# A windowed-attention transformer kernel: scores of four units made ahead of the attention loop, and the row maxima of two units taken in succession

## The reference, cut to what matters

```
x = x + attn0(layernorm(x))            # 16 heads of 16, causal over all 1024 tokens
x = x + two_layers(layernorm(x))       # DEPTH 2, this case's part
# one layer:
h = shift_token(x)
q, k, v = split(h @ wqkv)              # 8 heads of 64
q, k = rotary_xpos(l2norm(q) * qs, l2norm(k) * ks)
o = local_attention(q, k, v)           # windows of 128 tokens; each sees itself and the one before
x = x + o @ wo
h = layernorm(shift_token(x)) * lg + lb
a, g = split(h @ w1 + b1)              # 682 hidden
x = x + (a * gelu(g)) @ w2 + b2
```

## Time and profile before

| | us |
|---|---|
| median of 3 runs | 2295.97 (2294.08 to 2304.67) |
| the profiled execution: its own time | 2298.97 |
| its span, first to last instruction | 2296.1 |
| PE busy in the span | 1990.5 (87%) |
| DVE busy | 1457.9 (63%) |
| ACT busy | 1243.2 (54%) |
| POOL busy | 798.9 (35%) |

### The profile page before, as it was taken

The page is one execution under the profiler, slowest core; times in us unless marked ns, Lnnn a source line. Parts: engine busy times, 40 slices in busy tenths (PEclk is TensorE's granted clock), DMA queues, the critical chain, the costliest instruction groups (busy, mean ns, idle before and its releaser), DMA issues.

```text
span 2296.1 us, 36136 instructions
## 1 busy us (share of the span) xinstructions
PE 1990.5 (87%) x11968; PEld 1241.2 (54%) x11968; DVE 1457.9 (63%) x3942; ACT 1243.2 (54%) x2980; POOL 798.9 (35%) x663
## 2 busy tenths in 40 slices
PE   5566899999988746999999999989899999999998
PEld 3232233333322424667667667667667667667666
DVE  5457788888885435746756755746755755756754
ACT  1110666666667323754754764763754764764663
POOL 2223321122232335505505605614613613623620
PEclk9896899999999877999999999999999999999999
DMA  4645855554540552000000000011200000000000
GB/s 144 152 124 114 147 128 83 84 73 71 105 123 11 147 156 78 1 24 14 1 24 15 1 19 19 2 68 43 73 19 19 20 19 19 19 19 19 20 1 28
DMA packets 124455, 128.97 MB, mean 56 GB/s; under 512 B 50460, under 2 KB 101232, under 8 KB 123248
## 3 DMA queue, kind: packets, MB, share of 16 engines
q1 hardware_dynamic: 123696, 117.75, 22.2%
q0 software_dynamic: 576, 8.91, 1.0%
HBM read 75.51 MB, written 50.86 MB: 55 GB/s over the span
## 4 chain that ended last, share of the span: by engine, by line
PE 38%; DVE 10%; ACT 8%; issue 5%; POOL 2%; DMA 0%; DVEq 0%; SPq 0%; ACTq 0%; POOLq 0%
PE qkv_ps L1338 5%; PE s_ps L1439 4%; DVE rot_s L1886 4%; PE s_ps L1384 4%; PE pt_ps L1518 3%; PE o_ps L1518 3%; PE pt_ps L1452 3%; PE o_ps L1477 3%; ACT p_sb L1630 3%; DVE p_sb L1895 3%; PE s_ps L1397 2%; PE qkv_ps L1397 2%; PE pt_ps L1439 2%; PE o_ps L1439 2%; POOL inv_norm L1780 2%
## 5 line engine op out<-in xcount | busy, mean ns | idle before, releaser
L717 ACT ACTIVATE probs<-st_ps 128x512 f32<-128x512 f32 (+3 forms) x768 | 329.8, 494 | 166.7 <-PE st_ps L625 166.2
L1338 PE MATMUL qkv_ps<-w_qkv,x_parts 128*128 128x512 f32 x1152 | 308.6, 411 | 32.7 <-DVE x_parts L1860 23.6
L1630 ACT ACTIVATE p_sb<-p_sb,negmax 128x256 f32<-128x256 f32 (+1 forms) x512 | 249.2, 489 | 63.2 <-DVE negmax L1895 63.1
L610 PE MATMUL s_ps<-k_stack,q_stack 96*128 96x512 bf16 (+3 forms) x768 | 242.1, 346 | 41.3 <-DVE piece_negmax L762 25.7
L762 DVE CUSTOM_DVE_ANT_0 seen<-s_ps,causal 128x128 f32<-128x128 f32 (+3 forms) x512 | 233.6, 484 | 43.7 <-PE s_ps L610 43.5
L1338 PEld LDWEIGHTS qkv_ps<-w_qkv,x_parts 128*128 128x128 f32 x1152 | 211.9, 194 | 80.0 <-issue 38.5
L625 PE MATMUL st_ps<-q_stack,k_stack 98*128 98x512 bf16 (+3 forms) x768 | 240.8, 334 | 14.4 <-ACT probs L717 10.1
L1895 DVE CUSTOM_DVE_ANT_0 p_sb<-s_ps,band 128x256 f32<-128x256 f32 (+1 forms) x512 | 185.4, 401 | 89.3 <-PE s_ps L1384 85.5
L844 POOL TENSOR_SCALAR_AFFINE_SELECT probs<-probs 128x512 f32<-128x512 f32 x128 | 81.6, 637 | 415.4 <-ACT probs L717 415.4
L1788 POOL TENSOR_TENSOR rot_c<-qn,turn_by 128x512 f32<-128x512 f32 x128 | 178.6, 1415 | 130.8 <-PE turn_ps L1364 105.0
L1646 ACT COPY p_t<-pt_ps 128x512 f32<-128x512 f32 (+1 forms) x256 | 143.2, 559 | 127.6 <-PE pt_ps L1452 126.3
(11 more groups left out here) (146 smaller groups left out, 3487.5 us busy)
## 6 DMA issues: line engine op xcount, KB each, us to landing
qk_scratch<-parts SPq DMA_DIRECT2D x64, 192.0 KB, 2.8
q_stack<-qk_scratch SPq DMA_DIRECT2D x96, 128.0 KB, 6.7
k_stack<-qk_scratch SPq DMA_DIRECT2D x96, 128.0 KB, 7.1
w_ffn<-ffn_weights POOLq DMA_DIRECT2D x4, 2176.0 KB, 11.4
v_scratch<-v_out SPq DMA_DIRECT2D x32, 256.0 KB, 2.6
v_sb<-v_scratch SPq DMA_DIRECT2D x16, 512.0 KB, 10.3
x_in<-xt_scratch SPq DMA_DIRECT2D x16, 512.0 KB, 4.1
ffn_weights<-w_high SPq DMA_DIRECT2D x2, 2176.0 KB, 8.1
```

The source lines that it names most:

```text
L610: pe.matmul(s_ps[i % 3][:, 0:kw], q_stack[0:STK, slot, h, qt * P:(qt + 1) * P], k_stack[0:STK, slot, h, k0:k0 + kw], start=True, stop=True ...
L717: act.activation(probs[:, n % 3, h, q0:CH], st_ps[i % 3][:, q0:CH], ACT.Exp).then_inc(exp_done.sem, 1)
L1338: mm = pe.matmul(qkv_ps[:, part * CH:(part + 1) * CH], x_parts[:, w % XR, xp, k, :], w_qkv[:, wp, k, part * INNER:(part + 1) * INNER], sta ...
L1630: act.activation(p_sb[:, u % 4, h, k0:PW], p_sb[:, u % 4, h, k0:PW], ACT.Exp, scale=-1.0, bias=negmax[:, u % 4, h:h + 1], accum_out=total[ ...
```

## The change

Four things are done together.

1. EARLY becomes 4. The scores of group 1 (units 2 and 3), their maxima and their exponentials move from the loop to the end of the feed-forward (and the prologue of iteration 0).
2. What these need moves with them: the two turns of tile 1 on PE, their copies on ACT.
3. The projection of tile 3 (called tile four in the change's words, counted from one), part 0 and 1, follows right behind `down(1, 1)`, and part 2 comes at u = 2; `unit_vectors` and `times_sin` of tile 2, which the projection waits for, move on DVE to a place ahead of `output(1, 1)`. `square` and `copy_v` of tile 3 on ACT move to u = 0 and u = 2.
4. On DVE the maxima of two units stand in succession: at each even u `mask_scores(it, u)` and `mask_scores(it, u + 1)`, and ahead of `low_x` and `sums` instead of behind them.

```
-EARLY = 2
+EARLY = 4
 # PE, loop
-                    if p < 2 and w + 1 < NT:
+                    if p < 2 and 0 < w < NT - 1:
                         turn(it, w + 1, p)
...
+                    if u == 2:
+                        project(it, AHEAD, 2)
-                    if p >= 1 and w + AHEAD < NT:
+                    if p >= 1 and 0 < w < NT - AHEAD:
                         project(it, w + AHEAD, p - 1)
 # PE, end of the feed-forward (the prologue has the same)
                 if more:
                     scores(it + 1, 0)
                 down(1, 0)
+                if more:
+                    turn(it + 1, 1, 0)
+                    scores(it + 1, 1)
+                    turn(it + 1, 1, 1)
                 down(1, 1)
+                if more:
+                    for part in range(2):
+                        project(it + 1, AHEAD, part)
 # ACT
+            def first_exponentials(it):
+                for u in range(EARLY):
+                    if u >= 2:
+                        copy_turned(it, 1, u - 2)
+                    exponentials(it, u)
...
-                    if p < 2 and w + 1 < NT:
+                    if p < 2 and 0 < w < NT - 1:
                         copy_turned(it, w + 1, p)
...
-                    if p == 2 and w + AHEAD < NT:
+                    if p == (2 if w else 0) and w + AHEAD < NT:
                         square(it, w + AHEAD)
-                    if p == 3 and w + AHEAD < NT:
+                    if p == (3 if w else 2) and w + AHEAD < NT:
                         copy_v(it, w + AHEAD)
...
 # DVE, loop
+                    if EARLY <= u < UNITS and u % 2 == 0:
+                        mask_scores(it, u)
+                        mask_scores(it, u + 1)
                     if p == 2 and w + AHEAD + 1 < NT:
                         low_x(it, w + AHEAD + 1)
                     if p == 3 and w + AHEAD < NT:
                         sums(it, w + AHEAD)
-                    if EARLY <= u < UNITS:
-                        mask_scores(it, u)
...
-                    if p == 0 and w + 2 < NT:
+                    if p == 0 and 0 < w < NT - 2:
                         unit_vectors(it, w + 2)
-                    if p == 1 and w + 2 < NT:
+                    if p == 1 and 0 < w < NT - 2:
                         times_sin(it, w + 2)
 # DVE, end of the feed-forward (the prologue likewise)
                 if more:
                     mask_scores(it + 1, 0)
+                    mask_scores(it + 1, 1)
                     sums(it + 1, 2)
                 output(1, 0)
                 if more:
-                    mask_scores(it + 1, 1)
+                    mask_scores(it + 1, 2)
+                    mask_scores(it + 1, 3)
+                    unit_vectors(it + 1, 2)
+                    times_sin(it + 1, 2)
                 output(1, 1)
```

More of the change, by code:

```diff
@@ L1576, in _ @@
             scores(0, 0)
+            turn(0, 1, 0)
+            scores(0, 1)
+            turn(0, 1, 1)
+            for part in range(2):
+                project(0, AHEAD, part)
             for it in range(LAST):
@@ L1732, in feed_forward @@
                 if more:
-                    for u in range(EARLY):
-                        exponentials(it + 1, u)
+                    first_exponentials(it + 1)
             high_weights(0)
@@ L1746, in _ @@
                     copy_turned(0, 0, 1)
-            for u in range(EARLY):
-                exponentials(0, u)
+            first_exponentials(0)
             for it in range(LAST):
@@ L2065, in _ @@
                 mask_scores(0, u)
+            unit_vectors(0, 2)
+            times_sin(0, 2)
             for it in range(LAST):
```

## The result

The changed kernel takes 2293.62 us (median of 20 runs, 2285.82 to 2297.86). The kernel before, run beside it, takes 2300.80 (20 runs), some 5 us above the median shown ahead of the prediction. The ratio is 0.9967, 95% interval [0.9956, 0.9977]: 0.33% faster, less than the 0.5% that the prediction called a gain, and half of the 14.0 us forecast (which would be 0.9939). The time of 2293.62 lies 0.6 us outside the range.

The account below looks back on a forecast made before the run. PE's own work was taken to bound the kernel, leaving about 11 us idle per iteration. Seams 9.0 + 4.8, prologue 0.4, steady tiles 5.2, tail -5.4 gave 14.0 off 2295.97: 2282 us, range 2268 to 2293.

Parts of the forecast that it names:

- What bounds the kernel: Whole kernel: PE's own work bounds it, so all the change can win is PE's idle 11 us per iteration.
- the steady tiles: Tiles after the seam: loop falls from 13.0 to 12.3, under PE's 12.45; 0.65 us won per iteration, 5.2 in all.
- The split of the input in its new place: `low_x` on DVE, steady tiles: starts under POOL's add, ends 0.28 behind it, over 1.4 us rather than 0.41.
- The 0.5 of waiting for `qn`: Tile after the seam: `qn` late again by about 0.5 us, subtracted from the steady tiles' gain.
- The seam: Between iterations: 2.03 wait goes, 1.6 `qn` wait comes; 2.25 us won in iterations 1 to 4, 1.6 in 5 to 7.
- The tail: Iteration's end: unit 29's maximum delays the second half of `hn` by 0.69 us; 5.4 lost in all, bounds 0 to 5.5.
- The clock: New gap ahead of tile 4's projection: half clock given no term in the sum, kept only as a rival, chance 0.08.
- The sum: Whole kernel: seams 9.0 + 4.8, prologue 0.4, steady tiles 5.2, tail -5.4, together 14.0 us won.
- iteration 0's prologue: Ahead of iteration 0's tiles: bound by the same loop, 0.4 us won.
- All waits go: Rival, seam and steady tiles: all 3.77 us of waits per iteration won, 30 us, 2266; chance 0.15.
- The wait only moves: Rival, feed-forward: waits for `q_t` or `output(1, 1)` lose 1.2 us more per seam, 2290; chance 0.19.
- the slower one: Rival, new gap ahead of tile 4's projection: PE's clock falls once per iteration, 3.6 us each, 2311; chance 0.08.

Follow-up runs that it names:

- `unit29_late`: The changed kernel with only unit 29's maximum put back behind the second half of `hn`; 2293.29 us, 0.9960 of the kernel before.
- `tail_single`: The changed kernel with maxima in pairs only up to unit 23, each later one at its own place; 2282.12 us, 0.9927 of the kernel before.
- `filled`: The changed kernel plus 18 unread identity matmuls in PE's two gaps around tile 2's second turn; 2284.10 us, 0.9921 of the kernel before.

## Why the prediction was wrong

**What bounds the kernel, and the steady tiles: right, with one term mis-sized.** The waits of 0.59, 0.51 and 0.50 went, and the scores of tiles 4 and 5 start 12.4 behind the tile before where 12.45 was forecast; those of tile 3 start 12.71 behind. The split of the input in its new place took what the prediction read off, over 1.4 us rather than 0.41, and ended 0.28 behind POOL's add:

```profile
1277.84 1.51 DVE L1878 TENSOR_TENSOR x_parts<-x_in,x_parts 128x256 fp32r<-128x256 f32 x1
```

```profile
1276.68 2.39 POOL L1811 TENSOR_TENSOR rot_c<-rot_c,rot_s 128x1024 f32<-128x1024 f32 x1 [0.76 <-DVE rot_s L1904]
```

The Trainium skill's rule on the shared SBUF interfaces ("GPSIMD Engine Reference", section "Key points") held again: 1.51 under the add, 0.42 without one. The 0.5 of waiting for `qn` in the tile after the seam, which the sum had subtracted, did not come (the projection at 1273.05 has no wait), and in the second layer the wait in the seam itself is 0.89, in iterations 5 to 7. From the scores of tile 2 to those of tile 5 it is 38.57 us before and 37.53 after, in every iteration alike: 1.04, or 8.3 in all, where the sum had 5.2. The 0.5 was mis-sized, in the change's favour.

**The seam: right in its mechanism.** `down(1, 1)` ends at 1248.5 from 1237.14, 11.3 against 11.5 forecast. From the start of `down(1, 0)` the scores of tile 1 come 16.40 later (forecast 16.46), and the new wait for `qn` is 1.41 (1.6). `output(1, 1)` was late by its input and cost nothing. At full clock (iteration 1) the scores of tile 2 come 29.72 later (30.01), against 32.21 before: 2.5 won for a forecast of 2.25. In the second layer's seams at full clock (iterations 5 and 7) they come 29.84 later, against 32.42 and 32.08: 2.2 to 2.6 won for a forecast of 1.6.

**The tail: right mechanism, mis-sized.** The step "unit 29's maximum now stands ahead of the second half of `hn` ... 0.69 more" looked at one of the two maxima that pass the normalisation. Unit 27's stands ahead of the statistics; through POOL's `rstd` it delays the first half of `hn` by 0.43. It measured 1.13 x 8 = 9.0 us (0.69 and 0.43 split by `unit29_late`, the whole by `tail_single`) against 5.4, and outside the bounds of 0 to 5.5. In iteration 1 the tail loses 0.36 more, which no run explains.

**The clock: the step that failed.** The sum has no term for the half clock, so the forecast put it at nothing. The prediction kept it as a rival with 3.6 us in each iteration and a chance of 0.08, against it "the idle time is shorter than the one that is removed, and that one brought it only at times". It did come, at a smaller price: 1.5 us in four iterations, 5.9 us by `filled`, against 0.4 in three iterations of the kernel before. All or nothing was the wrong form. The row that should have warned stood in the earlier trace rows: scores at half clock behind a wait of 2.03. The idle time that replaced it, 0.76 and 1.41 with 0.6 us of turns between, is 2.17 in sum, no less. "Only at times" was three seams in seven, as the rows of iteration 1 above show. So the clock falls about as often as before, in four seams. What the change altered is what it falls on: a projection and scores, with no wait for `negmax` behind them. That this is why it costs more is read from the timelines; no run isolates it.

The Trainium skill's gate rule that the prediction cited ("TensorE: Matmul & The Clock Gate", "Part 1: The HAM clock gate") was applied to the mean: 0.99, before and after. The mean hides it, since 2.9 us of 174 at half the clock move it by 0.008. The same page, section "A second HAM failure mode: psum-queue depth-cycling", tells of another kernel, in bf16, in which short idle times between groups of matmuls make the clock go up and down. By that rule the trace agrees (0.50 granted behind 0.76 and 1.41), and `filled` shows that here the clock does not fall without them.

**Iteration 4: missed.** It lost 0.33 where 2.21 was to be won, although the slow `down` of the kernel before gave it 0.76; of the 3.3 missing, 1.5 are the half clock. For the rest see the waits ahead of it and POOL's timeline there (the load of the second layer's feed-forward weights is issued on POOL and waits for the last `down`):

```profile
1611.54 0.63 PE L1364 MATMUL turn_ps<-ident,rot_c 128*128 128x128 f32 x4 [1.88 <-ACT q_t L1636]
1614.28 2.90 PE L1338 MATMUL qkv_ps<-w_qkv,x_parts 128*128 128x512 f32 x6 [2.11 <-DVE qn L1890]
```

```profile
1601.82 1.18 POOL L1844 DMA_DIRECT2D w_ffn<-ffn_weights  x2 [3.73 <-PE pt_ps L1520]
1603.01 2.55 POOL L1806 TENSOR_TENSOR rot_c<-qn,turn_by 128x512 f32<-128x512 f32 x2
```

`unit_vectors` and `times_sin` of tile 2 now run ahead of `down(1, 1)`, but POOL's half of that rotation stands behind the load's issue, where POOL waits for 3.73 us (2.03 before), and its power for tile 3 behind that. The two waits are 1.1 and 0.7 longer than in iterations 2 and 3, and without the half clock, in `filled`, the scores of tile 2 come 2.0 later than there. I had not looked at what else stands in POOL's queue where the rotation was moved to. That the issue is the cause is read from the trace; no run moved the load.

**The sum, term by term.** Forecast 14.0, measured 9.4 from the attention's first turn to the end. The seven seams, from `down(1, 0)` to the scores of tile 2, won 8.7 for 13.8; the steady tiles 8.3 for 5.2; the tail lost 9.3 for 5.4; 0.8 is the `down` of iteration 3, which no term had and which ran at half clock for a shorter time than before, and 1.0 is iteration 0's prologue, for 0.4. That the steady tiles gave 3.1 more and the tail took 3.9 more, so that the two nearly cancel, is luck. The medians are 7.2 us apart; the parts of the span ahead of the attention, which differ by chance, are in them.

**Rivals and range.** "All waits go" did not come, for the reasons given. "The wait only moves" (2290) named waits for `q_t` in the feed-forward (0.44, less than before) or for `output(1, 1)` (none); neither came. By size the time is between that rival and the slower one, with the mechanism of the latter in half of the iterations and the larger tail.

## What to carry to other kernels

Where a long wait is taken away, add up the short ones that take its place close together: here two of 0.8 and 1.4 us with a little work between brought the half clock as one of 2.0 did, and it cost 1.5 us rather than 0.4. A few matmuls that nobody reads, put into such a gap, measure its price in one run. Look for the half clock by the times of single groups in every iteration, not in one iteration and not in the mean. When a loop's order is changed for its middle, walk its last rounds separately and list everything that each moved instruction passes: the two pairs in the last tile took back more than the pairs in the middle gave. An edit can move the half clock to other places and so hide its own gain, as `unit29_late` did, so compare iterations at full clock, and try repairs together before dropping one.

## What the runs showed of the hardware

- The clock's fall depends on more than the gap just ahead. In the kernel before, waits of 2.03 ahead of the scores of tile 1 brought it in iterations 1 and 2 and not in 3 and 4 (2.06 and 2.02), and waits of 1.70 in 5 and not in 6 and 7. In the changed kernel a wait of 1.41 left it up in iteration 1 and brought it down in 2 and 3; one of 0.89 left it up in 5 and 7 and brought it down in 6; two executions had this alike. Taking 0.69 us out of the tail, some 98 us ahead, changed the count from four to seven with the same waits in the seam.
- With waits of 0.95 and 1.56 one execution of the same kernel ran the projection in 1.60 and another in 2.90.
- A fall covered the projection and a quarter of the scores behind it (2.90 and 1.40 instead of 1.63 and 1.13), or all of both (2.90 and 2.08), though PE had no wait between them. It cost an iteration 1.4 to 1.5 us in the changed kernel and 0.4 in the kernel before.
- 18 additional matmuls per iteration, 2.3 us of PE's time in a gap, made the kernel 0.46% faster; they took away every half-clock stretch in the seams and left the one at the `down` of iteration 3.
